# Band matrices built in quarters inside the normalisation steps of the first two images

## The chip, the cores and the metric

The kernel runs on one core of a Trainium2 chip. The metric is the time of one execution on the device in microseconds (us); smaller is better. The engines of the core are TensorE (PE, with PEld for its weight loads), VectorE (DVE), ScalarE (ACT), GpSimd (POOL) and SyncE (SP), which here only issues DMAs. Each engine takes its instructions in the order in which they are written, and semaphores order them between engines.

## What is computed

One metaformer layer on `x` of shape (32, 112, 112, 96): a normalisation over the channels, a depthwise 3x3 convolution with a residual, then a second normalisation and a two-layer network (96 to 384 to 96) in rounded formats with a residual.

```python
x = x + _L0_conv_ref(_ln_c(x), L0_conv_kernel)     # conv 3x3, depthwise, SAME; returns y + its input
t = _to_tokens(x)
t = t + _L0_ffn_ref(_ln_t(t), W1, b1, W2, b2)      # relu between the layers, 8-bit inputs, 16-bit sums
x = _from_tokens(t, x)
```

The convolution is done on TensorE: for each channel and each of the three column shifts, a 112x112 band matrix holds the three vertical taps around its diagonal (with 1 added at the centre for the residual), and is multiplied with the image, whose rows lie on the partitions.

## The kernel before

Work goes in pairs of images (`IMGS = 2`). A chunk is 8 columns of one image, 14 chunks an image, so a pair has `UNIT = 28` chunks. A step handles one chunk in each stage of a pipeline. Step numbers `t` run from `NORM_AT - 1 = -31`. The normalisation of chunk e is at step e - 30, so steps -30 to -3 normalise the first pair. The convolution of that pair starts at step -2 (`CONV_AT`), the network at step 28 (`FFN_AT`), and after 32 the steady stretch runs in a loop of 56 steps. Every engine has a function `step(r, c, t)` that writes its part of a step, and `run` (on SP its own lines) calls it for all steps.

In a step that only normalises, SP loads the next chunk into one of two buffers `xn` once that buffer's last chunk has been normalised by both ACT and DVE. DVE computes moments (`statistics`, four `bn_stats`, L582), ACT the square root (`deviation`, L485), DVE the reciprocal and the negated mean (`invert`, L614, L618), and then DVE (`normalise`, L640) and ACT (L465) write four columns each into `images`.

Before the steps there is a setup. Weights are rounded and transposed, the taps are split into three bf16 parts, and then the 112 rows of the band matrices are made. TensorE multiplies shifted identities (`shift`) with the taps (L326) into one of three PSUM banks (two banks of `conv_ps`, and `y_ps`). A build, `n`, is one bank: 288 columns, in two matmuls of 144. There are 112 builds; even ones are copied to SBUF by DVE (L563), odd ones by ACT (L429). TensorE may be three builds ahead of the copies. The copies go to `band_stage`, which lies in the second half of `images` and holds one half of the channels at a time: after 56 builds SP stores it to `bands` in DRAM (L289, 7056 KB), the copies of the second half wait for that store, and after the other 56 builds the second store goes out. On DVE and ACT all 112 builds stand ahead of step -30. SP issues the loads of steps -31 and -30, then the first store, then the loads of the next two steps, then the second store, and then the rest. The first use of `bands` is SP's load of a band into `band_ring` (L277) at step -3, ahead of which SP waits for both stores; TensorE's first convolution matmul (L384) needs such a band. The chunk whose normalisation would overwrite `band_stage` is that of step -2 (`STAGED_FROM`), and it waits for the stores too.

Of the kernel before, what the change touches and what calls it, by code (L numbers as in the profile page):

```python
# [31 lines left out]
def metaformer(nc, x, conv_kernel, w1, b1, w2, b2, bands, out):  # L32
# [7 lines left out]
    NB = C * DX  # L40
# [5 lines left out]
    with ExitStack() as ctx:  # L46
# [6 lines left out]
        def sem(name):  # L53
# [36 lines left out]
        band_stage = images[:, 1, :, :, :].rearrange("p i c w -> p (i c w)")[:, 0:NB // 2 * H] \  # L90
            .rearrange("p (g n h) -> p g n h", g=GROUPS // 2, h=H)
# [27 lines left out]
        SETUP_COLS = 2  # L119
        SETUPS = H // SETUP_COLS  # L120
        band_ps = [bank[0:H, 0:SETUP_COLS * NB // 2] for bank in (conv_ps[:, 0], conv_ps[:, 1], y_ps)]
# [7 lines left out]
        bands_out = [sem(f"bands_out{i}") for i in range(2)]  # L129
# [43 lines left out]
        def dma_count(r, e, ring, per=LOOP):  # L173
            return (per // ring) * 16 * r + 16 * (e // ring + 1)

# [10 lines left out]
        with nc.Block() as block:  # L186
# [54 lines left out]
            def _(sp):  # L241
# [39 lines left out]
                first = NORM_AT - 1  # L281
                for half in range(2):
                    for c in range(first, first + 2):
                        step(0, c, c)
                    first += 2
                    for s in band_col:
                        sp.wait_ge(s, SETUPS // 2 * (half + 1))
                    lo = GROUPS // 2 * half
                    sp.dma_start(bands[lo:lo + GROUPS // 2].rearrange("g h n k -> h g n k"), band_stage) \  # L289
                        .then_inc(bands_out[half], 16)  # L290
                for c in range(first, LOOP_AT):
# [14 lines left out]
            def _(pe):  # L306
# [13 lines left out]
                for n in range(2 * SETUPS):  # L320
                    half, i = divmod(n, SETUPS)
                    if n >= 3:
                        pe.wait_ge(band_col[(n - 3) % 2], (n - 3) // 2 + 1)
                    for a in range(SETUP_COLS):
                        h = SETUP_COLS * i + a
                        mm = pe.matmul(band_ps[n % 3][:, NB // 2 * a:NB // 2 * (a + 1)],  # L326
                                       shift[:, H - 1 - h:2 * H - 1 - h],
                                       taps_16[:, NB // 2 * half:NB // 2 * (half + 1)], start=True, stop=True)
                    mm.then_inc(band_mm, 1)
                pe.wait_ge(w_copied, 2)  # L330
                for s in band_col:
                    pe.wait_ge(s, SETUPS)
# [36 lines left out]
                def conv(r, c, ch, next_waits):  # L369
# [3 lines left out]
                    if i == 0:  # L373
                        if g == 0:
                            for s in normed:
# [14 lines left out]
                def convs(r, c, t, lo, hi, next_waits=None):  # L390

                    chans = conv_channels(t)[lo:hi]
                    for ch in chans:
                        conv(r, c, ch, next_waits if ch == chans[-1] else None)
# [23 lines left out]
            def _(act):  # L418
# [5 lines left out]
                for n in range(1, 2 * SETUPS, 2):  # L424
                    i = n % SETUPS
                    act.wait_ge(band_mm, n + 1)
                    if n == SETUPS + 1:
                        act.wait_ge(bands_out[0], 16)
                    nc.scalar.activation(band_stage[:, :, :, SETUP_COLS * i:SETUP_COLS * (i + 1)],  # L429
                                         band_ps[n % 3].rearrange("p (h g n) -> p g n h", h=SETUP_COLS, n=TAPS),  # L430
                                         ACT.Identity).then_inc(band_col[1], 1)
# [82 lines left out]
            def _(dve):  # L514
# [43 lines left out]
                for n in range(0, 2 * SETUPS, 2):  # L558
                    i = n % SETUPS
                    dve.wait_ge(band_mm, n + 1)  # L560
                    if n == SETUPS:
                        dve.wait_ge(bands_out[0], 16)
                    dve.tensor_copy(band_stage[:, :, :, SETUP_COLS * i:SETUP_COLS * (i + 1)],  # L563
# [81 lines left out]
                def step(r, c, t):  # L645
# [3 lines left out]
                    if after or norm:  # L649
                        statistics(r, c, t)  # L650
                    if before:
# [38 lines left out]
```

## Time and profile before

| | |
|---|---|
| median of 3 runs | 4024.47 us |
| lowest and highest | 4016.77 and 4032.15 us |
| the profiled execution, its own time | 4024.61 us |
| its span, first to last instruction | 4022.9 us |
| busy: PE, DVE, ACT, POOL | 78%, 90%, 73%, 43% of the span |
| instructions | 87017 |

The profile is of one execution, and its time is 0.14 us above the median of the runs and 1.7 us above its span. The busy shares are means over stages with different limits, so the table doesn't say what one stage is worth; the views of the stretch up to the first convolution do. In the rows, a line such as L326 is a line of the kernel before. "Idle before" is the time an engine stood idle just before an instruction, with what ended it. The issue of a DMA is shown on SPq, and such a row's length is that of issuing when it holds one DMA, and of the stretch when it holds several.

### The profile page before, as it was taken

What the parts mean: (1) busy time and instruction counts of PE and PEld (TensorE: products, weight loads), DVE (VectorE), ACT (ScalarE), POOL (GpSimd) and SP (SyncE); (2) the same over time, 40 slices, a digit from 0 to 9 for tenths busy, and PEclk for the clock granted to TensorE, in tenths of its full rate; (3) what the DMA queues carried; (4) which work ended last, traced back from release to release, by engine and by line L of the source; (5) the groups of instructions that cost most, each with busy time, mean ns of one, the idle gap of its engine ahead of it and who ended that gap; (6) DMA issues with size and microseconds to landing.
All of it is one profiled execution on the core that took longest, in us unless ns stands there. A gap on an engine that the chain in (4) does not pass through costs nothing.

```text
span 4022.9 us, 87017 instructions
## 1 busy us (share of the span) xinstructions
PE 3152.2 (78%) x24678; PEld 2482.8 (62%) x24678; DVE 3613.3 (90%) x12635; ACT 2935.4 (73%) x6204; POOL 1720.4 (43%) x915
## 2 busy tenths in 40 slices
PE   3088888878888788888888888888888888889977
PEld 2077666666666666666666666666666666667744
DVE  4647999999999999999999999998999999999998
ACT  3456777777777777777777777777777777777765
POOL 0002444444444444444444444444444444445555
PEclk9999999999999999999999999999999999999955
DMA  4466666666666666666666666666666666665533
GB/s 146 114 170 172 188 188 185 187 184 187 187 185 189 177 190 190 182 180 185 188 185 188 185 186 188 185 188 183 187 189 186 188 185 196 191 191 172 160 106 94
DMA packets 277321, 714.60 MB, mean 178 GB/s; under 512 B 34777, under 2 KB 34882, under 8 KB 276802
## 3 DMA queue, kind: packets, MB, share of 16 engines
q1 hardware_dynamic: 276802, 708.57, 60.1%
q8 instruction: 217, 3.56, 0.4%
q14 instruction: 302, 2.47, 0.2%
HBM read 539.84 MB, written 168.59 MB: 176 GB/s over the span
## 4 chain that ended last, share of the span: by engine, by line
PE 55%; ACT 31%; issue 7%; DMA 5%; DVE 1%; ACTq 1%; SPq 0%; POOLq 0%; POOL 0%; DVEq 0%
PE conv_ps L384 33%; ACT images L465 14%; PE hid_ps L352 13%; ACT hid L444 9%; PE y_ps L365 7%; ACT xt L436 4%; ACT y L452 4%; DMA band_ring<-bands 2%; DMA xn<-in_x 2%; ACTq L167 1%; DMA bands<-images 1%; PE conv_ps L326 1%; DVE stats L582 0%; PE y_ps L326 0%; PE xt_ps L339 0%
## 5 line engine op out<-in xcount | busy, mean ns | idle before, releaser
L384 PE MATMUL conv_ps<-images,band_ring 112*112 112x222 f32 (+1 forms) x9216 | 2064.9, 363 | 604.9 <-ACT xt L436 385.2
L384 PEld LDWEIGHTS conv_ps<-images,band_ring 112*112 112x112 f32 x9216 | 1568.0, 179 | 896.7 <-issue 656.7
L444 ACT ACTIVATE hid<-hid_ps 128x896 f16<-128x896 f32 x1344 | 1226.3, 913 | 505.2 <-PE hid_ps L352 505.2
L224 POOL TENSOR_TENSOR xf<-xf,images 112x768 f32<-112x768 f32 x448 | 980.3, 2188 | 1299.2 <-DVE hid L571 893.7
L230 POOL TENSOR_TENSOR xf<-xf,y 112x768 f32<-112x768 f32 x448 | 736.8, 1645 | 999.3 <-DVE y L602 997.7
L626 DVE SCALAR_TENSOR_TENSOR xq<-xf,stats,xt_ps 112x96 fp8e5<-112x96 f32 x3584 | 844.3, 310 | 0.0
L365 PE MATMUL y_ps<-w2t,hid 128*128 128x96 f16 x10752 | 634.5, 211 | 173.8 <-ACT y L452 172.3
L365 PEld LDWEIGHTS y_ps<-w2t,hid 128*128 128x128 f16 x10752 | 555.1, 100 | 329.0 <-ACT y L452 213.3
L465 ACT ACTIVATE images<-xn,neg_mean,rstd 112x96 f32<-112x96 f32 x1792 | 723.0, 545 | 13.2 <-DVE neg_mean L618 13.2
L352 PE MATMUL hid_ps<-xt,w1t 96*128 96x448 fp8e5 x2688 | 695.6, 369 | 27.7 <-ACT xt L436 19.5
L452 ACT ACTIVATE y<-y_ps 112x384 f16<-112x384 f32 x896 | 443.8, 495 | 364.4 <-PE y_ps L365 362.9
L582 DVE BATCH_NORM_STATS2 stats<-xn 112x6 f32<-112x192 f32 x1792 | 513.5, 348 | 79.5 <-DMA xn<-in_x 77.1
L571 DVE TENSOR_SCALAR hid<-hid,b1q 128x896 f16<-128x896 f16 x1344 | 528.1, 446 | 19.5 <-issue 9.1
L582 DVE BATCH_NORM_STATS2 stats<-xf 112x6 f32<-112x192 f32 x1792 | 510.6, 347 | 0.0
L577 DVE TENSOR_SCALAR hid<-hid 128x2688 uint16<-128x2688 int16 x448 | 505.3, 1128 | 0.1
L640 DVE TENSOR_SCALAR images<-xn,stats,rstd 112x96 f32<-112x96 f32 x1792 | 486.2, 367 | 0.0
L475 ACT ACTIVATE images<-conv_ps 112x448 f32<-112x448 f32 x768 | 414.4, 540 | 79.7 <-PE conv_ps L384 75.4
L352 PEld LDWEIGHTS hid_ps<-xt,w1t 96*128 96x128 f16 x2688 | 263.5, 100 | 237.1 <-ACT hid L444 31.8
L612 DVE RECIPROCAL xt_ps<-std 112x8 f32<-112x8 f32 x448 | 93.5, 209 | 197.2 <-ACT std L485 197.1
L485 ACT ACTIVATE std<-stats,eps 112x8 f32<-112x8 f32 x896 | 225.1, 295 | 57.5 <-DVE stats L582 57.3
L602 DVE TENSOR_TENSOR y<-y,b2q 112x768 f16<-112x768 f16 x448 | 250.7, 559 | 6.7 <-ACT y L452 3.0
L436 ACT ACTIVATE xt<-xt_ps 128x448 uint16<-128x448 uint16 x448 | 235.5, 526 | 11.2 <-PE xt_ps L339 11.2
(46 smaller groups left out, 571.1 us busy)
## 6 DMA issues: line engine op xcount, KB each, us to landing
band_ring<-bands SPq DMA_DIRECT2D x768, 294.0 KB, 5.2
xn<-in_x SPq DMA_DIRECT2D x448, 336.0 KB, 3.5
xf<-in_x SPq DMA_DIRECT2D x448, 336.0 KB, 4.8
out<-xf SPq DMA_DIRECT2D x448, 336.0 KB, 3.9
bands<-images SPq DMA_DIRECT2D x2, 7056.0 KB, 24.5
xf<-in_L_ffn_W SPq DMA_DIRECT2D x2, 144.0 KB, 2.8
xf<-in_L_conv_kernel SPq DMA_DIRECT2D x3, 3.4 KB
xf<-in_L_ffn_b SPq DMA_DIRECT2D x1, 42.0 KB, 3.4
```

The costliest lines, as they stand in the source:

```text
L224: pool.tensor_tensor(x2, x2, images[:, b, i, :, cols].rearrange("p c w -> p w c"), ALU.add).then_inc(with_conv, 1)
L230: pool.tensor_tensor(res, res, y[:, c % 2], ALU.add).then_inc(summed, CW)
L352: mm = pe.matmul(hid_ps[:, k, u, 0:HALF * H], w1t[:, P * j:P * j + P], xt_8[0:C, c % 2, HALF // 2 * u:HALF // 2 * (u + 1)], start=True, st ...
L365: mm = pe.matmul(y_ps[:, C * w:C * w + C], hid[:, c % 2, TOK * j + tok:TOK * j + tok + P], w2t[:, j, :], start=(j == 0), stop=(j == J - 1))
L384: mm = pe.matmul(dst[:, :, lo:hi], band_ring[:, n % BAND_RING, PAIR * dx + i, :], images[:, m % 2, :, ch, lo + dx - 1:hi + dx - 1], start= ...
L444: nc.scalar.activation(hid[:, c % 2, TOK * j:TOK * (j + 1)].rearrange("p (u n) -> p u n", u=2), hid_ps[:, k, :, 0:HALF * H], ACT.Identity) ...
L452: nc.scalar.activation(y[:, c % 2, HALF * u:HALF * u + HALF, :], y_ps[0:H, 0:HALF * C].rearrange("p (w c) -> p w c", c=C), ACT.Identity).t ...
L465: op = nc.scalar.activation(images[:, b, i, :, cols.start + w], xn[:, e % NORM_RING, w, :], ACT.Identity, bias=neg_mean[:, c % 2, w:w + 1] ...
L571: dve.tensor_scalar(part_j, part_j, b1q[:, j:j + 1], None, ALU.add).then_inc(hid_biased, 1)
L577: dve.tensor_scalar(bits.bitcast(U16), bits.bitcast(I16), ROUND8, -ROUND8, ALU.add, ALU.add).then_inc(hid_quant, 1)
L582: op = dve.bn_stats(stats[:, c % 2, i, w:w + 2, :].rearrange("p w s -> p (w s)"), src[:, w:w + 2, :].rearrange("p w c -> p c w"))
L626: op = dve.scalar_tensor_tensor(out=xq_8[:, (c + 1) % 2, w // 2, 0:C, w % 2], in0=xf[0:H, e % FFN_RING, w, :], scalar=stats[:, c % 2, 0, w ...
```

## The change

The band matrices are made in quarters of the channels instead of halves. A build still fills one bank with 288 columns, now in four matmuls of 72 columns for four image rows, instead of two of 144. A quarter is 28 builds, and there are 112 builds as before. The builds leave the setup and go into the steps: five builds in each of steps -30 to -9 and two in step -8 (function `setups`). In a step, TensorE has its builds first. ACT has its odd builds first, ahead of the square root. DVE has its even builds behind `statistics` and ahead of `invert`. The staging area keeps its size and is now two buffers of a quarter each. SP stores a quarter (3528 KB) in the step in which its last build stands, behind that step's load: steps -25, -19, -14 and -8. TensorE waits for all copies only ahead of the first convolution.

```diff
+        QUARTERS = 4
+        QGROUPS = GROUPS // QUARTERS
+        QB = NB // QUARTERS
-        SETUP_COLS = 2
+        SETUP_COLS = 4
         SETUPS = H // SETUP_COLS
+        STEP_SETUPS = 5
...
+        def setups(c, t):
+            n = STEP_SETUPS * (t - NORM_AT)
+            return range(n, min(n + STEP_SETUPS, QUARTERS * SETUPS)) if c == t and n >= 0 else range(0)
...  SyncE
+                done = {(SETUPS * (q + 1) - 1) // STEP_SETUPS + NORM_AT: q for q in range(QUARTERS)}
+                for c in range(NORM_AT - 1, LOOP_AT):
                     if c == CONV_AT - 1:
                         for s in bands_out:
                             sp.wait_ge(s, 16)
                     step(0, c, c)
+                    if c in done:
+                        q = done[c]
+                        for s in band_col:
+                            sp.wait_ge(s, SETUPS // 2 * (q + 1))
+                        sp.dma_start(bands[QGROUPS * q:QGROUPS * (q + 1)].rearrange("g h n k -> h g n k"),
+                                     band_stage[:, q % 2]).then_inc(bands_out[q], 16)
...  TensorE
+                def build(n):
+                    q, i = divmod(n, SETUPS)
                     if n >= 3:
                         pe.wait_ge(band_col[(n - 3) % 2], (n - 3) // 2 + 1)
                     for a in range(SETUP_COLS):
                         h = SETUP_COLS * i + a
+                        mm = pe.matmul(band_ps[n % 3][:, QB * a:QB * (a + 1)], shift[:, H - 1 - h:2 * H - 1 - h],
+                                       taps_16[:, QB * q:QB * (q + 1)], start=True, stop=True)
                     mm.then_inc(band_mm, 1)
...  ScalarE
+                    for n in setups(c, t):
+                        if n % 2:
+                            build(n)
                     if now:
                         copy_xt(r, c)
...  VectorE
                     if after or norm:
                         statistics(r, c, t)
+                    for n in setups(c, t):
+                        if n % 2 == 0:
+                            build(n)
                     if before:
                         quantise(r, c - 1)
                     if after or norm:
                         invert(r, c, t)
```

What follows is the order of instructions on three engines. COPY and ACTIVATE `images<-conv_ps` or `images<-y_ps` are the copies of builds.

VectorE before, two of the normalising steps (-28 and -27):

```order
L582 BN_STATS stats<-xn 112x6 [waits xn_in0,normed_dve,normed_act]
L582 BN_STATS stats<-xn 112x6 x3
L614 RECIPROCAL rstd<-std 112x8 [waits std_done]
L618 SCALAR_TENSOR_TENSOR neg_mean<-stats,rstd 112x8 [waits rstd_done]
L640 TENSOR_SCALAR images<-xn,stats,rstd 112x96 x4
L582 BN_STATS stats<-xn 112x6 [waits xn_in1,normed_dve,normed_act]
```

VectorE now, steps -28 and -27:

```order
L593 BN_STATS stats<-xn 112x6 [waits xn_in0,normed_dve,normed_act]
L593 BN_STATS stats<-xn 112x6 x3
L574 COPY images<-conv_ps 112x72x4 [waits band_mm] x2
L574 COPY images<-y_ps 112x72x4 [waits band_mm]
L625 RECIPROCAL rstd<-std 112x8 [waits std_done]
L629 SCALAR_TENSOR_TENSOR neg_mean<-stats,rstd 112x8 [waits rstd_done]
L651 TENSOR_SCALAR images<-xn,stats,rstd 112x96 x4
L593 BN_STATS stats<-xn 112x6 [waits xn_in1,normed_dve,normed_act]
L593 BN_STATS stats<-xn 112x6 x3
L574 COPY images<-conv_ps 112x72x4 [waits band_mm] x2
L625 RECIPROCAL rstd<-std 112x8 [waits std_done]
```

Three copies and then two stand between the moments and the reciprocal, in turn from step to step; there were none.

ScalarE before, two of the same steps:

```order
L485 ACTIVATE std<-stats,eps 112x8 [waits stats_done]
L465 ACTIVATE images<-xn,neg_mean,rstd 112x96 [waits neg_done]
L465 ACTIVATE images<-xn,neg_mean,rstd 112x96 x3
L485 ACTIVATE std<-stats,eps 112x8 [waits stats_done]
L465 ACTIVATE images<-xn,neg_mean,rstd 112x96 [waits neg_done]
```

ScalarE now, steps -28 and -27:

```order
L437 ACTIVATE images<-y_ps 112x72x4 [waits band_mm]
L437 ACTIVATE images<-conv_ps 112x72x4 [waits band_mm]
L493 ACTIVATE std<-stats,eps 112x8 [waits stats_done]
L473 ACTIVATE images<-xn,neg_mean,rstd 112x96 [waits neg_done]
L473 ACTIVATE images<-xn,neg_mean,rstd 112x96 x3
L437 ACTIVATE images<-conv_ps 112x72x4 [waits band_mm]
L437 ACTIVATE images<-y_ps 112x72x4 [waits band_mm]
L437 ACTIVATE images<-conv_ps 112x72x4 [waits band_mm]
L493 ACTIVATE std<-stats,eps 112x8 [waits stats_done]
```

The square root of a step now stands behind two or three copies, of which each waits for TensorE.

SyncE's queue before, from the first loads of chunks to the first load of a band:

```order
L262 DMA xn<-in_x 112x768 x2
L289 DMA bands<-images 112x24x672 [waits band_col_act,band_col_dve]
L262 DMA xn<-in_x 112x768 [waits normed_dve,normed_act] x2
L289 DMA bands<-images 112x24x672 [waits band_col_act,band_col_dve]
L262 DMA xn<-in_x 112x768 [waits normed_dve,normed_act] x24
L262 DMA xn<-in_x 112x768 [waits normed_act,normed_dve,bands_out1,bands_out0]
L277 DMA band_ring<-bands 112x672 x2
```

SyncE's queue now, the same place:

```order
L270 DMA xn<-in_x 112x768 x2
L270 DMA xn<-in_x 112x768 [waits normed_dve,normed_act] x5
L299 DMA bands<-images 112x12x672 [waits band_col_act,band_col_dve]
L270 DMA xn<-in_x 112x768 [waits normed_dve,normed_act] x6
L299 DMA bands<-images 112x12x672 [waits band_col_act,band_col_dve]
L270 DMA xn<-in_x 112x768 [waits normed_dve,normed_act] x5
L299 DMA bands<-images 112x12x672 [waits band_col_act,band_col_dve]
L270 DMA xn<-in_x 112x768 [waits normed_dve,normed_act] x6
L299 DMA bands<-images 112x12x672 [waits band_col_act,band_col_dve]
L270 DMA xn<-in_x 112x768 [waits normed_dve,normed_act] x4
```

Two stores of 24 groups of channels are now four of 12, with five or six loads of chunks between them.

## Rows read from the trace of the kernel before

**Rows 1.** Stages: start:end, length, busy us (instructions) by engine, clock, DMA, GB/s

```profile
13.30:32.90 19.60, 19.37 (x116) 14.83 (x117) 13.33 (x32) 11.55 (x28) 0.00 (x0) 1.00 0.00 1
32.90:57.00 24.10, 0.46 (x4) 0.23 (x2) 0.04 (x1) 0.04 (x1) 0.00 (x0) 1.00 0.86 300
57.00:75.60 18.60, 17.88 (x106) 13.57 (x106) 12.60 (x28) 11.19 (x28) 0.00 (x0) 1.00 0.01 1
...
109.10:189.40 80.30, 0.00 (x0) 0.00 (x0) 57.94 (x234) 44.28 (x116) 0.00 (x0) 1.00 0.35 95
360.00:3820.00 3460.00, 2823.37 (x22797) 2247.20 (x22796) 3236.26 (x11409) 2650.49 (x5591) 1598.99 (x834) 0.99 0.63 185
```

**Rows 2.** Chain that ended last, pieces in order: start us, us, what

```profile
32.90 23.97 DMA bands<-images
...
86.52 22.44 DMA xn<-in_x
...
193.93 4.51 PE conv_ps L384 x12
```

**Rows 3.** Timeline, setup and step -30: start us, us, engine, what [idle before]

```profile
13.69 0.20 DVE L557 CAST b2q<-xf 112x96 f16<-112x96 fp8e5 x1
...
19.93 0.46 DVE L563 COPY images<-conv_ps 112x288 f32<-112x288 f32 x1 [0.29 <-PE conv_ps L326]
...
20.44 0.74 PE L326 MATMUL conv_ps<-xf 67*112 67x144 bf16 x4
20.46 0.46 DVE L563 COPY images<-y_ps 112x288 f32<-112x288 f32 x1
20.97 0.41 ACT L429 ACTIVATE images<-conv_ps 112x288 f32<-112x288 f32 x1 [0.33 <-PE conv_ps L326]
...
20.98 0.49 PE L326 MATMUL y_ps<-xf 67*112 67x144 bf16 x2
...
75.61 1.14 DVE L582 BATCH_NORM_STATS2 stats<-xn 112x6 f32<-112x192 f32 x4
75.96 1.28 ACT L485 ACT_TABLE_LOAD   x1
...
82.87 0.38 SPq L289 DMA_DIRECT2D bands<-images  x1
82.90 1.15 DVE L582 BATCH_NORM_STATS2 stats<-xn 112x6 f32<-112x192 f32 x4 [1.12 <-DMA xn<-in_x]
```

**Rows 4.** Timeline of steps -26 to -24, columns as in rows 3

```profile
109.07 1.15 DVE L582 BATCH_NORM_STATS2 stats<-xn 112x6 f32<-112x192 f32 x4 [19.93 <-DMA xn<-in_x]
110.26 0.30 ACT L485 ACTIVATE std<-stats,eps 112x8 f32<-112x8 f32 x1 [20.46 <-DVE stats L582]
110.59 0.20 DVE L614 RECIPROCAL rstd<-std 112x8 f32<-112x8 f32 x1 [0.37 <-ACT std L485]
...
111.03 1.62 ACT L465 ACTIVATE images<-xn,neg_mean,rstd 112x96 f32<-112x96 f32 x4 [0.47 <-DVE neg_mean L618]
111.87 1.14 DVE L582 BATCH_NORM_STATS2 stats<-xn 112x6 f32<-112x192 f32 x4
...
116.05 1.15 DVE L582 BATCH_NORM_STATS2 stats<-xn 112x6 f32<-112x192 f32 x4 [1.26 <-DMA xn<-in_x]
```

**Rows 5.** Timeline of step -4, columns as in rows 3

```profile
185.31 1.15 DVE L582 BATCH_NORM_STATS2 stats<-xn 112x6 f32<-112x192 f32 x4 [1.01 <-DMA xn<-in_x]
```

**Rows 6.** DMA issues by line, 0 to 420 us: KB each, median us to landing

```profile
xn<-in_x SPq DMA_DIRECT2D x67, 336.0 KB, 3.5
```

**Rows 7.** Short stretch inside the first store, columns as in rows 1

```profile
37.00:50.00 13.00, 0.00 (x0) 0.00 (x0) 0.00 (x0) 0.00 (x0) 0.00 (x0) 1.00 1.02 356
```

More of the change, by code:

```diff
@@ L118, in metaformer @@
         b2_8 = staged(H, C).bitcast(F8)[:, 0:C]
-        SETUP_COLS = 2
+        SETUP_COLS = 4
         SETUPS = H // SETUP_COLS
-        band_ps = [bank[0:H, 0:SETUP_COLS * NB // 2] for bank in (conv_ps[:, 0], conv_ps[:, 1], y_ps)]
+        STEP_SETUPS = 5
+        band_ps = [bank[0:H, 0:SETUP_COLS * QB] for bank in (conv_ps[:, 0], conv_ps[:, 1], y_ps)]
         w1_in, w2_in, small_in, taps_sem = sem("w1_in"), sem("w2_in"), sem("small_in"), sem("taps_in")
@@ L128, in metaformer @@
         band_col = [sem("band_col_dve"), sem("band_col_act")]
-        bands_out = [sem(f"bands_out{i}") for i in range(2)]
+        bands_out = [sem(f"bands_out{i}") for i in range(QUARTERS)]
         xn_in = [sem(f"xn_in{i}") for i in range(NORM_RING)]
@@ L278, in step @@
                                 .then_inc(band_in[n % BAND_RING], 16)
[L281 to L291, printed above, removed]
+                done = {(SETUPS * (q + 1) - 1) // STEP_SETUPS + NORM_AT: q for q in range(QUARTERS)}
+                for c in range(NORM_AT - 1, LOOP_AT):
                     if c == CONV_AT - 1:
@@ L319, in _ @@
                 pe.wait_ge(prep, 31)
-                for n in range(2 * SETUPS):
-                    half, i = divmod(n, SETUPS)
+                pe.wait_ge(w_copied, 2)
+                def build(n):
+                    q, i = divmod(n, SETUPS)
                     if n >= 3:
@@ L367, in ffn2, with conv @@
                     mm.then_inc(y_mm, 1)
-                def conv(r, c, ch, next_waits):
+                def conv(r, c, t, ch, next_waits):
                     m = (c - CONV_AT) // UNIT
@@ L374, in conv @@
                         if g == 0:
+                            if t == CONV_AT:
+                                for s in band_col:
+                                    pe.wait_ge(s, QUARTERS * SETUPS // 2)
                             for s in normed:
@@ L393, in convs @@
                     for ch in chans:
[L394 removed]
+                        conv(r, c, t, ch, next_waits if ch == chans[-1] else None)
                     if next_waits and not len(chans):
@@ L423, in _, with build @@
                                      ACT.Identity).then_inc(w_copied, 1)
-                for n in range(1, 2 * SETUPS, 2):
-                    i = n % SETUPS
+                def build(n):
+                    q, i = divmod(n, SETUPS)
                     act.wait_ge(band_mm, n + 1)
-                    if n == SETUPS + 1:
-                        act.wait_ge(bands_out[0], 16)
-                    nc.scalar.activation(band_stage[:, :, :, SETUP_COLS * i:SETUP_COLS * (i + 1)],
+                    if q >= 2 and i == 1:
+                        act.wait_ge(bands_out[q - 2], 16)
+                    nc.scalar.activation(band_stage[:, q % 2, :, :, SETUP_COLS * i:SETUP_COLS * (i + 1)],
                                          band_ps[n % 3].rearrange("p (h g n) -> p g n h", h=SETUP_COLS, n=TAPS),
@@ L557, in _, with build @@
                 dve.tensor_copy(b2q[:, :], b2_8).then_inc(prep, 1)
-                for n in range(0, 2 * SETUPS, 2):
-                    i = n % SETUPS
+                def build(n):
+                    q, i = divmod(n, SETUPS)
                     dve.wait_ge(band_mm, n + 1)
-                    if n == SETUPS:
-                        dve.wait_ge(bands_out[0], 16)
-                    dve.tensor_copy(band_stage[:, :, :, SETUP_COLS * i:SETUP_COLS * (i + 1)],
+                    if q >= 2 and i == 0:
+                        dve.wait_ge(bands_out[q - 2], 16)
+                    dve.tensor_copy(band_stage[:, q % 2, :, :, SETUP_COLS * i:SETUP_COLS * (i + 1)],
                                     band_ps[n % 3].rearrange("p (h g n) -> p g n h", h=SETUP_COLS, n=TAPS)) \
@@ L650, in step @@
                         statistics(r, c, t)
+                    for n in setups(c, t):
+                        if n % 2 == 0:
+                            build(n)
                     if before:
```

10 lines of the change are left out of this document (2 added, 8 removed).

## Prediction, made before the changed kernel was run

> **What bounds the kernel now.** I read the stages first [rows 1], because the change touches only what stands ahead of the first convolution. In the steady stretch, 360 to 3820 us, VectorE is busy 3236 of 3460 us, and its code is the same before and after. What can move is when the first convolution starts, at 193.93 us [rows 2]. If nothing behind it changes, all that follows shifts by as much.
>
> Up to there I read the chain of waits and the timeline. The builds run by themselves from 13.3 to 32.9 us and from 57.0 to 75.6 us. Between them every engine stands still for the first store, 23.97 us [rows 1, 2]. Normalisation starts only at 75.61 us [rows 3]. Step -28 starts at 82.90 us, together with the second store (issued at 82.87 us) [rows 3]. The loads behind it on the same queue wait: one issued at 86.52 us takes 22.44 us instead of the usual 3.5 us [rows 2, 6], so step -26 starts at 109.07 us [rows 4]. From step -24 at 116.05 us to step -4 at 185.31 us nothing disturbs: 69.26 us for 20 steps, 3.46 us a step [rows 4, 5]. There a step is bound by its loads: VectorE is busy only 57.94 of 80.3 us [rows 1]. The work of one chunk takes 2.80 us of VectorE's time from moments to the next moments (109.07 to 111.87) [rows 4].
>
> **What is removed.** VectorE is done with the small setup at 13.89 us (13.69 + 0.20), and the moments of step -30 can start at about 13.85 instead of 75.61 us [rows 3]: 61.8 us less, the two build stretches and the exposed store. The stall of the second store goes too: without it step -26 would have started 6.94 us after step -28, at 89.84 us, so 19.2 us of the wait until 109.07 go. Together 81.0 us.
>
> **What the builds cost in a step.** VectorE gains two or three copies of 0.46 us behind the moments, ScalarE two or three of 0.41 us ahead of the square root, TensorE five builds. TensorE needs no data of the step and has three builds ready when a step begins, but no more: build n waits for the copy of n-3. One hand-over therefore falls into each step. Take a step whose first build n is even. ScalarE copies n+1 while VectorE still computes moments. Its next copy, n+3, needs TensorE's build n+3, which needs VectorE's copy of n, and that stands behind the moments. I go along this in time from the start of the moments:
> - moments until 1.14, copy of n from about 1.13 to 1.59;
> - TensorE, then ScalarE's copy. In the setup the copy that frees the bank ended at 20.39 us, TensorE started at 20.44 us and ScalarE at 20.97 us [rows 3]: 0.58 us for two matmuls (the four matmuls of that row are two builds). The two more cost 0.10 to 0.13 us each (0.74 us for four in a row, 0.49 for two), less 0.06 us since the last is 72 columns narrower: 0.75 us. ScalarE copies from 2.34 to 2.75;
> - the square root at 2.75, and the reciprocal 0.33 us later (110.26 to 110.59) [rows 4], at 3.08. Before, it stood at 1.52 (109.07 to 110.59).
>
> That is 1.56 us more. In such a step VectorE's third copy, of build n+4, ends at about the same time or 0.1 us later. Where n is odd, ScalarE's last copy waits in the same way for VectorE's first one, with the same sum. So a step takes 2.80 + 1.6 = 4.4 to 4.5 us; I take 4.45. The load no longer bounds it. ScalarE's half of the normalising ends 3.58 us after the start of the moments (111.03 + 1.62 - 109.07), now 5.2 us, and the load needs 3.5 us more; 8.7 us fit into two steps of 4.45. The extra over the 3.46 us of before is 0.99 us in each of the 22 steps with five builds: **21.8 us**. The load of ScalarE's table, 1.28 us in step -30 [rows 3], hid in part behind the moments and now stands behind copies: **0.9 us** more.
>
> **What the stores cost.** Each of the four is issued in its step 1.7, 1.3, 2.8 and 1.6 us after the moments begin, when the quarter's last copy is done, and behind the load of the next chunk. So the next step has its data. The load for the step after that is behind the store. Before, 26.2 us passed from the issue of the store to the moments that waited for such a load (82.87 to 109.07) [rows 3, 4]. Half the bytes take between 13.1 us (all of it halves) and 16.1 us (only the bytes at the full rate: 356 GB/s [rows 7] move 3.61 MB in 10.1 us). A load of 336 KB takes 3.5 us [rows 6], of which its bytes are 1.0, so 2.5 us are fixed, and the bytes of loads behind the store, another 1 us, don't halve either: (26.2 - 3.5)/2 + 3.5 = 14.9. I take 15.0. The stall is that plus the store's place in the step, less two steps that go on meanwhile: for the first three together 3 x 15.0 + 5.8 - 6 x 4.45 = 24.1 us. The last is followed by short steps: 15.0 + 1.6 - (3.3 + 3.5) = 9.8 us. Together **33.9 us**. The stores end by step -6, so SyncE's wait at step -3 is free, and the wait for a staging buffer two quarters later ends long before (a store lands after some 14 us; its buffer is needed some 30 us on).
>
> The Trainium skill has a rule against such a split. Its page "DMA: Bandwidth & Descriptors", section Bandwidth, gives 78% of the peak for transfers of 1 MB and 97% for 16 MB, so a smaller transfer pays its fixed part again. An estimate from these two figures gives a fixed part of the length of 0.27 MB, 0.75 us at the rate of this trace, and 1.5 us for two more transfers. The row of the load says 2.5 us each, 5.0 us in all, and my sum has that in it; by the page the time would be some 3.5 us shorter. No row here shows a store of a quarter.
>
> **Sum.** 81.0 - 21.8 - 0.9 - 33.9 = 24.4 us gained. The first convolution would start near 169.5 us. The profiled execution took 4024.6 us, which is the median of the runs too: 4024.6 - 24.4 = **4000 us**. The bounds: a step of 4.35 to 4.75 us moves it by -2 to +7 us, a store of 13.1 to 16.1 us by -8 to +4 us. Its own range, with the runs' spread (they lie up to 8 us from their median), is 3988 to 4011 us.
>
> **Rivals.**
> - *The builds hide almost wholly.* VectorE is idle 28% of the undisturbed stretch, and its 2.5 copies add 1.1 us to 2.8, which would be 3.9 us a step if ScalarE's last copy never came late. Against it stands the order: the square root is behind that copy. Extra 0.45 us a step instead of 0.99 gives 12 us more, but each stall of a store grows by 1.1 us where it overlaps shorter steps: 3992 us; with no extra at all, 3984 us.
> - *Two hand-overs in a step.* If ScalarE's first copy comes so late that it too is waited for, another copy and another 0.75 us lie in a row behind the moments: 1.2 us more, a step of 5.6 us. The extra is then 22 x 2.14 = 47.1 us, and the first three stalls shrink by 2.3 us each: 75 us against 81 gained, 4018 us. For it: ScalarE ends the normalising of a step 0.7 us after the next moments have begun, and its copies start only then. Against it: 0.7 + 0.41 us is still ahead of the end of VectorE's first copy at 1.59.
> - *Slower: one build at a time.* If TensorE's lead is lost and every build waits for the copy just before it, a build costs 0.58 + 0.46 = 1.04 us and a step 2.8 + 5.2 = 8.0 us. That is 22 x 4.5 = 100 us, while the first three stalls nearly vanish (1 us each) and the last stays: 114 us with the table's load, against 81 gained, **4057 us**. It decides from a step of 6.0 us on (22 x 2.5 us and stores of 25 us). Against it speak the three banks: in the setup TensorE makes two builds in one go, and 58 builds take 19.6 us, 0.34 us each [rows 1, 3].
> - *The first convolution starts earlier and the gain doesn't arrive*, since the stretch from 190 to 360 us, bound by TensorE and loads of bands, or the loop starts in another rhythm. Nothing in the profile speaks for it; time within 20 us of before.
>
> **Chances.** Forecast 0.68, hidden 0.12, two hand-overs 0.10, slower 0.04, gain lost 0.06. This kernel's measurement tells 0.5%, 20 us, from no change; the border is 4004.4 us and cuts through the forecast's own range, so I put 0.13 of its 0.68 at same. Faster: 0.55 + 0.12 + 0.01 = 0.68. Same: 0.13 + 0.10 + 0.05 = 0.28. Slower: 0.04. The range that leaves out no more than two in ten is 3984 to 4013 us.
>
> **What the profile after would show.** Moments of step -30 near 13.9 us. Steps of 4.4 to 4.5 us, with the reciprocal 3.1 us behind the start of the moments and the square root right behind ScalarE's last copy; a square root that starts before it, or steps of 3.9 or 5.6 us, would give a rival right. Four waits of moments for a load, each some 6 to 10 us long; four copies idle for a store would be wrong. First convolution matmul at 169.5 us, give or take 8. If it starts there and the time isn't 20 to 28 us shorter, the step that failed is that the rest only shifts.

## The result and the profile after

| | before | after |
|---|---|---|
| median of 6 runs each | 4019.97 us | 3991.69 us |
| lowest and highest | 4012.52 to 4032.15 us | 3986.89 to 4000.73 us |
| span of the profiled execution | 4022.9 us | 3985.2 us |
| first convolution matmul | 193.93 us | 164.32 us |

The ratio is 0.9929, with a 95% interval of 0.9909 to 0.9948: 28.3 us faster by the medians, a little more than the 24.4 us of the forecast. The changed kernel was run again later, beside other runs of the kernel before, and gave 3993.32 us against 4023.71 us, a ratio of 0.9928 (0.9909 to 0.9946).

The chain of waits of the changed kernel, up to the first convolution, answers to [rows 2] (start us, us, what; the pieces between are the steps' own work):

```profile
40.73 11.61 DMA xn<-in_x
...
73.99 11.75 DMA xn<-in_x
...
103.27 12.20 DMA xn<-in_x
...
135.82 12.71 DMA xn<-in_x
...
160.07 4.12 DMA band_ring<-bands
164.32 4.05 PE conv_ps L390 x12
```

Up to the first convolution there is no DMA of `bands<-images` on the chain any more. In its place stand four loads of a chunk that took 11.6 to 12.7 us, where the loads have a median of 3.3 us. The timeline of VectorE and of SyncE's queue at these four places (start us, us, engine, what, idle before and what ended it), to be read beside [rows 3, 4]:

```profile
13.66 1.14 DVE L593 BATCH_NORM_STATS2 stats<-xn 112x6 f32<-112x192 f32 x4
...
37.35 0.33 SPq L299 DMA_DIRECT2D bands<-images  x1
...
52.46 1.15 DVE L593 BATCH_NORM_STATS2 stats<-xn 112x6 f32<-112x192 f32 x4 [7.85 <-DMA xn<-in_x]
...
70.30 0.48 SPq L299 DMA_DIRECT2D bands<-images  x1
...
85.86 1.15 DVE L593 BATCH_NORM_STATS2 stats<-xn 112x6 f32<-112x192 f32 x4 [7.95 <-DMA xn<-in_x]
...
100.93 0.32 SPq L299 DMA_DIRECT2D bands<-images  x1
...
115.59 1.15 DVE L593 BATCH_NORM_STATS2 stats<-xn 112x6 f32<-112x192 f32 x4 [8.91 <-DMA xn<-in_x]
...
133.75 0.32 SPq L299 DMA_DIRECT2D bands<-images  x1
...
148.65 1.15 DVE L593 BATCH_NORM_STATS2 stats<-xn 112x6 f32<-112x192 f32 x4 [9.12 <-DMA xn<-in_x]
```

From the issue of a store to the moments that waited behind it: 15.1, 15.6, 14.7 and 14.9 us, against 26.2 us for a store of twice the size.

One step with builds, -28, whose first build is even (the same columns; the last row is the next step's start):

```profile
23.27 1.14 DVE L593 BATCH_NORM_STATS2 stats<-xn 112x6 f32<-112x192 f32 x4
...
24.33 0.80 DVE L574 COPY images<-conv_ps 112x288 f32<-112x288 f32 x2
24.82 0.59 PE L333 MATMUL conv_ps<-xf 67*112 67x72 bf16 x4 [2.38 <-DVE images L574]
25.22 0.57 PE L333 MATMUL y_ps<-xf 67*112 67x72 bf16 x4
25.45 0.41 ACT L437 ACTIVATE images<-conv_ps 112x288 f32<-112x288 f32 x1 [1.16 <-PE conv_ps L333]
...
25.76 0.29 ACT L493 ACTIVATE std<-stats,eps 112x8 f32<-112x8 f32 x1
25.82 0.46 DVE L574 COPY images<-y_ps 112x288 f32<-112x288 f32 x1 [0.69 <-PE y_ps L333]
26.20 0.19 DVE L625 RECIPROCAL rstd<-std 112x8 f32<-112x8 f32 x1
...
27.47 1.14 DVE L593 BATCH_NORM_STATS2 stats<-xn 112x6 f32<-112x192 f32 x4
```

The hand-over is there to see. VectorE copies behind the moments, TensorE starts 0.05 us after the first copy's end (24.33 + 0.44) and was idle for 2.38 us until then, ScalarE and then VectorE wait for its result, and the reciprocal follows 2.93 us after the moments' start; before it was 1.52. The step takes 4.20 us. The steps whose first build is odd take 4.09 to 4.15, and the four steps from 19.18 to 35.83 us take 4.16 us on average.

### The profile page after: what moved, and what is told of

It is laid out like the page before. It is cut to its first block, busy times and chain, and to the rows that moved or that the text cites. A ratio compares the mean times of both kernels' runs of the same rounds, so it can differ in the third digit from the quotient of the medians.

```text
span 3985.2 us, 87474 instructions
## 1 busy us (share of the span) xinstructions
PE 3157.9 (79%) x24902; PEld 2493.7 (63%) x24902; DVE 3609.6 (91%) x12635; ACT 2925.6 (73%) x6204; POOL 1719.3 (43%) x915
## 4 chain that ended last, share of the span: by engine, by line
PE 54%; ACT 31%; issue 7%; DMA 4%; DVE 1%; ACTq 1%; SPq 1%; POOL 0%; POOLq 0%; DVEq 0%
PE conv_ps L390 33%; ACT images L473 14%; PE hid_ps L355 13%; ACT hid L452 9%; PE y_ps L368 7%; ACT y L460 4%; ACT xt L444 4%; DMA band_ring<-bands 3%; DMA xn<-in_x 1%; ACTq L171 1%; DVE stats L593 0%; PE conv_ps L333 0%; PE xt_ps L342 0%; DVE images L574 0%; SPq L270 0%
## 6 DMA issues: line engine op xcount, KB each, us to landing
bands<-images SPq DMA_DIRECT2D x4, 3528.0 KB, 13.6
```

## Experiments

Each theory was judged mainly by the start of the first convolution matmul, which shows changes of a microsecond that a median of a few runs doesn't. Whether it may be used so was the first question.

### The changed kernel a second time

> The changed kernel once more, for a second profile. It is to tell how much of the gain lies ahead of the first convolution matmul. Theory (pure shift): the first convolution matmul is at 164.3 us again, within 0.5 us, 29.6 us earlier than before, and from there to the end it takes between 3821 us (the first profile of the changed kernel) and 3829 us (the profile of before), with no systematic difference; ratio 0.993. Rival: the stretch behind it is shortened too, and is again near 3821 us, 8 us less than before, with a time near 3987 us.

Measured: first convolution matmul at 164.25 us, and 3828.7 us from there to the end of the span (3992.9), where the first profile has 3820.9 and the kernel before 3829.0. So the prologue repeats to 0.1 us, and the change shortens nothing behind it: pure shift. The 8 us by which the first profile was better belong to that execution. The stretch of the first convolution alone already shows it (start:end, length, busy by engine, granted clock, DMA share, GB/s). Before, then the changed kernel, then the changed kernel again:

```profile
193.90:349.70 155.80, 132.37 (x613) 118.18 (x614) 78.65 (x307) 78.22 (x199) 4.37 (x2) 0.91 0.60 166
```

```profile
164.30:314.50 150.20, 128.04 (x613) 114.16 (x614) 78.38 (x306) 79.37 (x202) 4.42 (x2) 0.94 0.63 175
```

```profile
164.20:320.90 156.70, 134.85 (x612) 119.26 (x612) 78.68 (x307) 78.36 (x200) 4.38 (x2) 0.90 0.62 169
```

The same work takes 150.2 us at a mean granted clock of 0.94 of full speed, and 155.8 and 156.7 us at 0.91 and 0.90. Since one changed execution is on each side, it isn't an effect of the change.

### One part alone: quarters, with all builds ahead

```diff
-            return range(n, min(n + STEP_SETUPS, QUARTERS * SETUPS)) if c == t and n >= 0 else range(0)
+            return range(0)
...  TensorE, ahead of the steps (VectorE the even, ScalarE the odd ones)
+                for n in range(QUARTERS * SETUPS):
+                    build(n)
...  SyncE, behind the first two steps
+                for q in range(QUARTERS):
+                    for s in band_col:
+                        sp.wait_ge(s, SETUPS // 2 * (q + 1))
+                    sp.dma_start(bands[QGROUPS * q:QGROUPS * (q + 1)].rearrange("g h n k -> h g n k"),
+                                 band_stage[:, q % 2]).then_inc(bands_out[q], 16)
```

> One part alone: quarters and two staging buffers as in the change, but all builds ahead of the normalising steps, as before. Theory (only the sum of the exposed pieces counts, and a store behind which builds go on costs nothing): builds at 0.34 us each, the third quarter waits for the first store (landing near 36.5 us) and the fourth for the second (near 48 us), so builds end near 57 us; then undisturbed steps of 3.46 us and one stall of some 8 us for the last store. First convolution matmul near 164 us, the same as with the whole change, time near 3991 us. Rival (it is the interleaving with the steps that wins): the quarters alone leave the stalls exposed, first convolution matmul at 178 us or later, time 4005 us or more.

Measured: first convolution matmul at 165.33 us; 3991.82 us, ratio 0.9931 (0.9910 to 0.9952). Its timeline shows what is left of the exposed stores (columns as above):

```profile
37.77 0.46 DVE L587 COPY images<-y_ps 112x288 f32<-112x288 f32 x1 [2.88 <-DMA bands<-images]
...
48.52 0.46 DVE L587 COPY images<-conv_ps 112x288 f32<-112x288 f32 x1 [0.47 <-DMA bands<-images]
...
73.93 1.15 DVE L609 BATCH_NORM_STATS2 stats<-xn 112x6 f32<-112x192 f32 x4 [8.93 <-DMA xn<-in_x]
```

In the kernel before, the same wait was this one:

```profile
56.96 0.46 DVE L563 COPY images<-y_ps 112x288 f32<-112x288 f32 x1 [24.40 <-DMA bands<-images]
```

The wait of 24.4 us has become 2.9 and 0.5 us, since two quarters can be in the staging area; one stall behind the last store remains. This version is 1.0 us later at the first convolution than the change, so the whole gain but 1 us is had without moving a single build into a step. The theory stands and the rival falls. In the steps, the builds cost 0.7 us a step and expose four stores to the loads; ahead of them, they cost 45 us once (58.73 - 13.66) and expose one store. The two come out equal here, and only as long as the stores are exposed: without the 2.9, 0.5 and 8.9 us of its waits this version would start the first convolution at 153.0 us (an estimate, 165.33 - 12.3), and the versions below that keep the builds in the steps and shrink the stores' stalls reach 134.96 us and less. Builds ahead of the steps with small stores or with stores in pieces were not run.

The builds themselves cost a little more in matmuls of 72 columns. Of the 45.1 us, 41.7 are left without the two waits; before, it was 61.95 - 24.40 = 37.6 us for the same 112 builds, 0.04 us less for each.

### Six banks instead of three

```diff
-        band_ps = [bank[0:H, 0:SETUP_COLS * QB] for bank in (conv_ps[:, 0], conv_ps[:, 1], y_ps)]
+        band_ps = [bank[0:H, 0:SETUP_COLS * QB] for bank in (conv_ps[:, 0], conv_ps[:, 1], y_ps,
+                   hid_ps[:, 0, 0], hid_ps[:, 0, 1], hid_ps[:, 1, 0])]
+        BANKS = len(band_ps)        # and BANKS in place of 3 in the ring
```

> The changed kernel with six PSUM banks for builds instead of three (three of the network's, which are unused then), so all five builds of a step can be made before it starts. Theory (one hand-over VectorE, TensorE, ScalarE stands ahead of the square root in each step, and sets it): steps with builds go from 4.15 to about 3.8 us, where the loads bound them; the four stalls grow by 0.7 us each; first convolution matmul near 159 us, time 5 us less than the changed kernel. Rival (the copies' own time on VectorE and ScalarE sets the step): steps stay at 4.1 us and the first convolution matmul at 164 us.

Measured: first convolution matmul at 154.72 us; 3987.51 us, ratio 0.9904 (0.9883 to 0.9925). Its step -28:

```profile
22.17 1.15 DVE L595 BATCH_NORM_STATS2 stats<-xn 112x6 f32<-112x192 f32 x4 [0.80 <-DMA xn<-in_x]
...
23.24 0.44 DVE L576 COPY images<-hid_ps 112x288 f32<-112x288 f32 x1
23.36 0.30 ACT L495 ACTIVATE std<-stats,eps 112x8 f32<-112x8 f32 x1 [0.80 <-DVE stats L595]
...
24.33 0.19 DVE L627 RECIPROCAL rstd<-std 112x8 f32<-112x8 f32 x1
...
25.60 1.15 DVE L595 BATCH_NORM_STATS2 stats<-xn 112x6 f32<-112x192 f32 x4
```

The square root starts 0.04 us after the moments, the reciprocal 2.16 us after their start and a step takes 3.43 us, or 4.0 to 4.4 where it waits for its load again. The hand-over was what set the step. The gain of 9.6 us is more than the 5 us expected, in part for two reasons that the trace shows. Step -30 takes 4.60 us instead of 5.52, since ScalarE's table is loaded earlier; and behind a stall two loads are ready at once, so that the four steps from 49.45 to 63.85 us take 3.60 us each and not the 3.8 us that I gave to steps bound by their loads. By the medians this version is 4 us faster than the change (3987.51 against 3991.69), and the two intervals overlap, so the 9.6 us show in the trace and not in the whole time.

### The square root ahead of ScalarE's copies

```diff
-                    for n in setups(c, t):          # first thing in ScalarE's step
-                        if n % 2:
-                            build(n)
...
                     if ffn_in(t + 1) or norm:
                         deviation(r, c, t)
+                    for n in setups(c, t):
+                        if n % 2:
+                            build(n)
```

> The changed kernel with ScalarE's square root ahead of its copies of a step instead of behind them; VectorE unchanged. Theory (in steps whose first build is odd, ScalarE's last copy delays the square root; in the others VectorE's third copy is as late anyway): steps with an odd first build fall to about 3.5 us, the others stay at 4.2, or the loads hold both at a mean of 3.9 us; first convolution matmul near 160 us. Rival (ScalarE's order doesn't matter): steps stay at 4.09 and 4.20 us, first convolution matmul at 164 us.

Measured: steps of 4.10 and 4.20 us and the first convolution matmul at 164.29 us, as the rival said; the one execution took 3986.72 us. But the reason isn't that the hand-over is absent. Step -27, whose first build is odd:

```profile
26.56 1.15 DVE L593 BATCH_NORM_STATS2 stats<-xn 112x6 f32<-112x192 f32 x4
27.62 0.44 DVE L574 COPY images<-conv_ps 112x288 f32<-112x288 f32 x1
27.74 0.30 ACT L493 ACTIVATE std<-stats,eps 112x8 f32<-112x8 f32 x1 [0.40 <-DVE stats L593]
...
28.39 0.96 PE L333 MATMUL conv_ps<-xf 67*112 67x72 bf16 x8 [2.38 <-ACT images L437]
29.02 0.46 DVE L574 COPY images<-conv_ps 112x288 f32<-112x288 f32 x1 [0.96 <-PE conv_ps L333]
...
29.40 0.19 DVE L625 RECIPROCAL rstd<-std 112x8 f32<-112x8 f32 x1
```

The square root is now done at 28.04, but ScalarE's first copy comes behind it, TensorE waits for that one, and VectorE's last copy, which stands ahead of the reciprocal, waits for TensorE. The hand-over has changed hands and costs the same. Taking it off one engine's queue doesn't help while the other's order still has it in front of the reciprocal. Of what was tried, only more banks helped; VectorE's copies behind the reciprocal were not tried. Step -30 got shorter, 4.19 us instead of 5.52, and the first two stalls took most of that back: 8.6 and 8.7 us instead of 7.9 and 8.0.

### Stores of a twelfth

```diff
-                        sp.dma_start(bands[QGROUPS * q:QGROUPS * (q + 1)].rearrange("g h n k -> h g n k"),
-                                     band_stage[:, q % 2]).then_inc(bands_out[q], 16)
+                        sp.dma_start(bands[QGROUPS * q:QGROUPS * q + 1].rearrange("g h n k -> h g n k"),
+                                     band_stage[:, q % 2, 0:1]).then_inc(bands_out[q], 16)
...
-                            sp.dma_start(band_ring[:, n % BAND_RING], bands[ch // PAIR]) \
+                            sp.dma_start(band_ring[:, n % BAND_RING], bands[ch // PAIR // QGROUPS * QGROUPS]) \
```

> The changed kernel with stores of one group of channels out of each twelve (294 KB instead of 3528 KB); the convolution then loads each quarter's first band every time, so eleven twelfths of the stores are left out and the output isn't the reference's. It measures the stores' cost by itself. Theory (a store costs what its bytes delay the load behind it): the four waits of 7.9 to 9.1 us shrink to under 1 us each, steps with builds stay near 4.15 us, first convolution matmul near 131 us, 33 us earlier than 164.3. Rival (the waits were those of the builds or of the loads' own latency): more than 10 us of the four waits stay, first convolution matmul at 140 us or later.

Measured: first convolution matmul at 129.85 us, no wait of moments for a load above 0.6 us in the steps with builds, and steps of 4.1 to 4.2 us but for the first and two in which a store is issued (4.37 us in step -25 and 4.75 in step -19); 3962.75 us in one execution. The moments behind the first store, which waited 7.85 us in the change, and the first convolution:

```profile
44.45 1.15 DVE L593 BATCH_NORM_STATS2 stats<-xn 112x6 f32<-112x192 f32 x4
```

```profile
129.85 4.26 PE conv_ps L390 x12
```

The stores of the change cost 34.5 us (164.32 - 129.85) more than stores of a twelfth.

### Stores in pieces

```diff
+        PIECES = 4
...
-                    if c in done:
-                        q = done[c]
-                        for s in band_col:
-                            sp.wait_ge(s, SETUPS // 2 * (q + 1))
-                        sp.dma_start(...)                       # the whole quarter
+                    for q, first in ((q, t) for t, q in done.items() if 0 <= c - t < PIECES):
+                        if c == first:
+                            for s in band_col:
+                                sp.wait_ge(s, SETUPS // 2 * (q + 1))
+                        lo, n = QGROUPS // PIECES * (c - first), QGROUPS // PIECES
+                        sp.dma_start(bands[QGROUPS * q + lo:QGROUPS * q + lo + n].rearrange("g h n k -> h g n k"),
+                                     band_stage[:, q % 2, lo:lo + n]).then_inc(bands_out[q], 16)
```

> The changed kernel with each quarter's store cut into four of three groups (882 KB), issued in four steps that follow one another (16 stores in all). Theory (a step of 4.15 us moves 1.5 MB at 356 GB/s, and a load and a piece are 1.25 MB, so a piece issued behind one load is gone before the next is issued): the waits for loads nearly vanish in steps with builds, and stay at 1 us in the last three pieces' shorter steps; first convolution matmul near 133 us, time near 3960 us. Rival (each transfer's fixed 2.5 us is paid on the path): 12 further transfers cost as much as they hide, first convolution matmul at 155 us or later.

Measured: first convolution matmul at 134.96 us; 3960.56 us, ratio 0.9851 (0.9831 to 0.9870). The same bytes as in the change, in four times as many stores, cost 5.1 us instead of 34.5 (134.96 - 129.85). A piece lands in a median of 5.6 us. At 356 GB/s [rows 7] its bytes take 2.5 us of that and those of a load ahead of it 1.0, so some 2 us are a fixed part (an estimate), and it is paid each time, but beside the steps and for the most part not on the path. Its issues up to 125 us (KB each, median us to landing):

```profile
bands<-images SPq DMA_DIRECT2D x16, 882.0 KB, 5.6
xn<-in_x SPq DMA_DIRECT2D x27, 336.0 KB, 3.5
```

### Whole quarters on ScalarE's DMA queue

```diff
...  ScalarE, first thing in its step; SyncE's store is gone
+                    if c == t and c - 1 in done:
+                        q = done[c - 1]
+                        for s in band_col:
+                            act.wait_ge(s, SETUPS // 2 * (q + 1))
+                        act.dma_start(bands[QGROUPS * q:QGROUPS * (q + 1)].rearrange("g h n k -> h g n k"),
+                                      band_stage[:, q % 2]).then_inc(bands_out[q], 16)
```

> The changed kernel with the four stores of whole quarters issued by ScalarE on its own DMA queue, at the start of the next step, and the loads left on SyncE's. Theory (it is the place in one queue that makes a load wait, not the bytes as such): a load and a store then share the DMA engines in turn, a load takes twice its 3.3 us at most, and the four waits shrink from 8 us to under 3 us each; first convolution matmul between 133 and 144 us, time near 3965 us. Rival (the DMA engines are simply full and the store's bytes go first, whatever the queue): the waits stay at 8 us and the first convolution matmul at 164 us.

Measured: first convolution matmul at 151.85 us; 3983.49 us, ratio 0.9906 (0.9890 to 0.9923). Neither theory: the four waits shrink from 7.9 to 9.1 us to 4.9 to 5.6 us, not to under 3.

```profile
39.20 0.35 ACTq L498 DMA_DIRECT2D bands<-images  x1
...
49.26 1.15 DVE L594 BATCH_NORM_STATS2 stats<-xn 112x6 f32<-112x192 f32 x4 [4.90 <-DMA xn<-in_x]
...
52.51 1.62 ACT L468 ACTIVATE images<-xn,neg_mean,rstd 112x96 f32<-112x96 f32 x4 [0.47 <-DVE neg_mean L630]
53.91 1.15 DVE L594 BATCH_NORM_STATS2 stats<-xn 112x6 f32<-112x192 f32 x4 [0.43 <-DMA xn<-in_x]
```

So each stall is 3 to 4 us shorter, and some 5 us remain although the load is on a queue of its own. The run changes two things, the queue and the time of issue: the store goes out at 39.20 us and not at 37.35. From the issue to the moments that waited it is now 10.1 us instead of 15.1. What the later issue does by itself was not tested. The issues between 39 and 55 us have three loads with a median of 8.4 us to landing, two and a half times what one takes alone. The Trainium skill says in "DMA: Bandwidth & Descriptors", section Queues, rings and completion order, that each engine serves the queues in turn, packet by packet. By that rule, with half of the bytes' rate for each queue, a load's 1 us of bytes would have become 2 and its 3.3 us some 4.3 (an estimate). The trace doesn't agree: it was 8.4 us, and the runs don't show why the store got more.

### Pieces and six banks

The edits of the runs with six banks and with pieces together.

> Both remedies: sixteen pieces as in the run with pieces, and six PSUM banks. Theory (two independent costs of the change, the hand-over in a step and the stall behind a store): steps with builds near 3.75 us, and the pieces fit less well, since 3.75 us is close to what a load and a piece need, so 0 to 0.5 us of wait in 16 steps; first convolution matmul near 126 us, time 38 us less than the changed kernel, near 3954 us. Rival (with shorter steps the pieces delay each load and take back what the banks give): first convolution matmul at 133 us or later, no better than with pieces alone.

Measured: first convolution matmul at 124.92 us; 3955.74 us, ratio 0.9835 (0.9814 to 0.9855), the fastest of all versions, 36 us less than the changed kernel's 3991.69 us. Where it waits, up to 120 us (us in total, times, longest):

```profile
DVE stats L597 <- DMA xn<-in_x: 15.1, 14, 2.1
```

The waits for loads are back, but small: 15.1 us in 14 places, where pieces alone had 5.1 us in 9. Ten microseconds at the first convolution are the banks' gain (134.96 - 124.92). By the medians it is 5 us, and the two intervals overlap, so what the banks add to the pieces shows in the trace up to the first convolution and not yet in the whole time. The profiled execution of this kernel had a mean granted clock of 0.964, that of pieces alone 0.967.

## Why the prediction was right, point by point

**The direction, the size and the cause.** 3991.69 us lies in the range of 3984 to 4013 and 8 us below the 4000. The gain was to be 24.4 us, and is 29.6 us at the first convolution and 28.3 us by the medians. So of the 8 us some 4 are gain, and the rest is that the kernel before now has a median of 4019.97 us, where the forecast was taken from 4024.6. By my chances "faster" had 0.68.

**What is removed: 81.0 us.** Moments of step -30 start at 13.66 us instead of 75.61 us: 61.95 us, forecast 61.8. The 19.2 us of the second store's stall are the prediction's own; no run shows them apart.

**The builds in a step: 21.8 us forecast, about 15.4 measured** (22 x 0.70, from 4.16 and 3.46 us). The mechanism is the one named: one hand-over per step, confirmed by the run with six banks. The step of the working that was mis-sized is the 4.45 us. Counted along step -28: VectorE's copy starts 1.06 us after the moments and not 1.13, and ends 0.02 us earlier still (0.44 us long); from its end to ScalarE's start it is 0.68 us and not 0.75; and the square root starts 0.31 us after the start of ScalarE's copy, not 0.41. The first and the last of these are the same slip: I added durations, where an instruction starts before the one ahead of it on its engine has ended (0.31 us behind the start of a copy of 0.41 on ScalarE, 0.36 behind one of 0.44 on VectorE). The one in between, 0.68 instead of 0.75, is TensorE's four matmuls. The reciprocal stands 2.81 us after the moments' start where the first build is odd and 2.93 where it is even, instead of 3.08 and a little more. Four matmuls of 72 columns take 0.57 to 0.59 us, 0.09 to 0.10 from one to the next, the low end of what I gave. Put into the prediction's own sum, a step of 4.16 us gives 24.4 + 16 x 0.29 = 29.0 us, since 6 of the 22 steps go on beside a stall; the error in this one term is nearly all that the forecast missed. For the same reason the bound for a step of 4.75 us was +5 and not +7 us.

**ScalarE's table: 0.9 us forecast.** The first step took 5.52 us, 1.36 more than the mean of the four behind it; before, it took 3.26, 0.46 more than the 2.80 us of a step that waits for nothing. That makes 0.9 us.

**The stores: 33.9 us forecast, 34.5 measured** with stores of a twelfth. The term rested on 15.0 us from issue to the moments, between 13.1 and 16.1; it was 14.7 to 15.6. The six steps that go on beside the first three stores took 25.85 us in the run with stores of a twelfth, not 26.7, which adds 0.85 us, and the stores were issued 1.5, 1.2, 2.7 and 1.5 us into their steps, 0.5 us less in sum than forecast, which takes half of it back.

**Sum of the terms:** 81.1 - 15.4 - 0.9 - 34.5 = 30.3 us, 0.7 us from the 29.6 of the trace. What is left over lies with the builds: the run with stores of a twelfth gains 64.1 us, so by it builds and table cost 17.0 us together, not 16.3. The two builds of step -8, which the forecast left out, are in these 17.0.

**The rest only shifts:** shown by the second profile, 3828.7 us behind the first convolution against 3829.0; the first profile's 3820.9 goes with its granted clock (last section).

**The rule against splitting.** I read the Trainium skill too widely. Its page "DMA: Bandwidth & Descriptors", section Bandwidth, asks for transfers of at least 1 MiB, and a quarter of 3528 KB is one. What I worked out, from its shares of the peak at 1 and 16 MB, was an estimate of 0.75 us a transfer. The trace doesn't agree: 7056 KB landed in 24.0 us, and 3528 KB in 13.0 us with nothing ahead (the first store of the run with builds ahead) and in a median of 13.6 in the change. So twice the bytes cost 10.4 to 11.0 us more, and a fixed part of 2.0 to 3.2 us is left, as the prediction's 2.5 had it. The measurement decides. That fixed part is in the 15.0 us. Whether a split is paid for depends on where: as four exposed stalls it was, as sixteen pieces between loads it was hidden.

**Rivals.** Steps of 3.9 or 3.46 us (hidden): no, 4.16, though with six banks it comes near. Two hand-overs in a step, or one build at a time: no, ScalarE's first copy was done before VectorE's first in steps -28, -27 and -26 (in step -28 at 24.29 against 24.77 us). Gain lost behind the first convolution: no.

**What the forecast missed** is not in its sum: it compared the change with the kernel before only. Builds ahead of the steps with the same quarters give the same time. So the change's gain can be had from the quarters and the second staging buffer alone, which end the 24 us wait and halve the bytes behind the last store, and moving the builds into the steps, as the change does it, swaps one cost for another. It pays once the stores are cut up (134.96 us against an estimated 153.0 for builds ahead with no wait for a store).

## What to carry to other kernels

When work is moved from a serial stretch into the gaps of a pipeline, count the hand-overs between engines that its order puts ahead of the pipeline's own chain, and give it as many buffers as a step has pieces. Here a store of 3528 KB on the queue of the loads held the moments up until some 15 us after its issue, less the two steps that went on meanwhile. Cut into pieces that fit between two loads, the stores cost 5.1 us instead of 34.5, even if every piece pays its fixed part. And test the parts of a change alone, then with its worst cost taken out: here the part that looked like its point, the builds inside the steps, brought 1 us as long as the stores were whole, and some 18 us, by the estimate above, once they were in pieces.

## What the runs showed of the hardware that I had not expected

The spread between executions, some 12 us of 3990 behind the first convolution, goes with the time that TensorE spends at the lower of its two clock levels (1.2 instead of 2.4 GHz) during short dips. The mean granted clock of the span and the time behind the first convolution, over ten profiled executions of nine kernels with the same instructions there (the run with stores of a twelfth loads other bands): at 0.967 it took 3820.7 to 3823.4 us (four executions), at 0.966 3828.1 to 3829.0 us (three), at 0.964 to 0.965 3831.2 to 3832.6 us (three). In all ten the clock is low for the last 200 us or so, so that isn't what differs. The dips before that add up to 58 to 61 us in the first four executions, 68 to 75 in the next three and 79 to 82 in the last three: each microsecond more at the low level goes with about half a microsecond more. It is so within one kernel too: the six executions of the changed kernel took 3986.9 and 3987.3 us at 0.967, 3990.8 to 3995.7 at 0.966 and 4000.7 at 0.965. Two of the kernels, the one with pieces and the one with pieces and six banks:

```profile
core 0: 3957.1 us, clock 0.967
```

```profile
core 0: 3957.5 us, clock 0.964
```

The second started its first convolution 10 us earlier and ended at the same time. A difference of a few microseconds between two single executions of this kernel means nothing until both clocks have been looked at, while the start of the first convolution repeats to 0.1 us (164.32 and 164.25).

The row of the granted clock doesn't tell the clock from the start. Three stretches of TensorE's convolution matmuls in the kernel before (columns as in rows 1):

```profile
193.90:197.90 4.00, 3.97 (x11) 3.39 (x12) 2.66 (x11) 0.30 (x1) 0.00 (x0) 1.00 0.44 123
205.60:211.00 5.40, 5.40 (x15) 4.54 (x16) 2.52 (x10) 0.93 (x3) 0.00 (x0) 0.50 0.44 121
212.70:216.00 3.30, 3.30 (x19) 3.11 (x18) 1.38 (x6) 1.21 (x4) 0.00 (x0) 1.00 0.68 191
```

The first goes at the pace of the second: the matmuls of both have a median of 579 ns and their weight loads of 310, where the third has 351 and 177. Yet the row says 1.00 for the first and 0.50 for the second. So TensorE was at the lower level when the convolution began, although the row doesn't show it. The builds ahead of it look the same: a weight load of 112 columns in bf16 takes a median of 210 ns in them (L326) and a wider one, of 128, takes 97 ns in the steady stretch (L339, 1007 to 1300 us), where the rows say 1.00 and 0.99. In each of the ten traces the record of the clock begins only behind the first convolution matmul. The fall to 0.50 of the second stretch came while TensorE stood idle for 2.48 us, waiting for a band.
